# Gathers of a graph attention kernel issued for two edge tiles at a time

## The reference

```python
# reference(), shortened
xn = _layernorm(x, axis=-1)
x = x + gnn(xn, src, dst, ...) + mix(xn[None], ...)[0]
x = x + ffn(_layernorm(x, axis=-1)[None], ...)[0]

# gnn: N = 3125 nodes, 103125 edges sorted by dst, H = 4 heads of D = 64
q = (feat @ Wq).reshape(N, H, D)
k = (feat @ Wk).reshape(N, H, D)
v = (feat @ Wv).reshape(N, H, D)
e = jnp.einsum('ehd,ehd->eh', k[src], q[dst]) / sqrt(H * D)
ex = jnp.exp(e - segment_max(e, dst)[dst])
a = ex / segment_sum(ex, dst)[dst]
ft2 = segment_sum(v[src] * a[..., None], dst).reshape(N, F)
rst = _layernorm(ft2 + feat, ln_g, ln_b)
...                       # two layers with a leaky unit, a second layernorm
# mix: per head of 32 features, sums over tokens of products of pairs of
# normalised k with v, then the same pairs of normalised q against them
# ffn: router, top 2 of 8 experts, gelu(xe @ W1 + b1) @ W2 + b2
```

## Time and profile before

| | |
|---|---|
| median of 3 runs | 2643.17 us |
| lowest and highest | 2631.5 and 2644.66 us |
| the profiled execution, its time | 2620.13 us |
| its span in the profile | 2618.4 us |
| TensorE clock granted, mean share of full speed | 0.851 |
| busy in the span: PE, DVE, ACT, POOL | 2074.0, 1757.7, 1479.9, 1215.0 us |
| first and last gather of the edges start | 107.7 and 1726.5 us |

### The profile page before, as it was taken

One profiled execution on the slowest core, in us unless ns is written; L12 is line 12 of the kernel. 1 busy time (PEld: TensorE's weight loads), 2 busy tenths in 40 slices (PEclk: granted clock), 3 DMA queues, 4 the chain that ended last, 5 costly groups with the idle time before them and its releaser, 6 DMA issues. The chain is left out here.

```text
span 2618.4 us, 45726 instructions
## 1 busy us (share of the span) xinstructions
PE 2074.0 (79%) x12641; PEld 1454.6 (56%) x12641; DVE 1757.7 (67%) x3515; ACT 1479.9 (57%) x4918; POOL 1215.0 (46%) x1183
## 2 busy tenths in 40 slices
PE   7747777777786667778777777857989986999998
PEld 3423333333332255556555555545778876999997
DVE  7457777777777676676667566677979985444443
ACT  2246555665665636566566555666865534555554
POOL 0456555555566445555555555524820001444443
PEclk9868788888888758787888877867989987999999
DMA  7666666666666556666666556647920118222221
GB/s 215 201 181 201 189 187 183 197 186 194 186 195 198 173 161 178 175 191 177 195 177 192 176 169 196 188 125 228 313 95 25 31 42 288 38 35 35 33 36 20
DMA packets 227731, 406.06 MB, mean 155 GB/s; under 512 B 58972, under 2 KB 129809, under 8 KB 227521
## 3 DMA queue, kind: packets, MB, share of 16 engines
q0 software_dynamic: 83712, 250.84, 34.5%
q1 hardware_dynamic: 120852, 116.88, 14.9%
q10 hardware_dynamic: 22957, 35.95, 3.7%
HBM read 345.66 MB, written 58.83 MB: 154 GB/s over the span
## 5 line engine op out<-in xcount | busy, mean ns | idle before, releaser
L826 POOL DMA_INDIRECT ring<-kv_tab,idx x904 | 918.4, 1016 | 709.0 <-issue 361.3
L1170 ACT ACTIVATE val<-ring,val 128x64 f32<-128x64 f32 x1808 | 477.2, 342 | 8.2 <-DVE part L928 7.3
L885 DVE TENSOR_TENSOR ring<-ring,tile_bank 128x1024 f32<-128x1024 f32 x226 | 274.4, 1214 | 64.5 <-ACT tile_bank L1160 41.6
L890 DVE TENSOR_REDUCE score<-ring 128x16 f32<-128x1024 f32 x226 | 268.3, 1212 | 0.0
L922 DVE TENSOR_TENSOR val<-val 128x1040 f32<-128x1040 f32 x113 | 140.3, 1242 | 184.0 <-ACT val L1170 174.5
L1286 PE MATMUL tile_bank<-q_win,spread 128*128 128x256 f32 x452 | 176.2, 476 | 108.3 <-DVE val L914 50.6
L2240 POOL DMA_INDIRECT out<-e_yw,to_row x56 | 120.7, 2155 | 222.3 <-DVE e_yw L2267 206.1
L2316 PE MATMUL e_h<-e_xT,e_now 128*128 128x128 f32 x1792 | 211.9, 277 | 0.7 <-DVE e_now L2257 0.7
L2316 PEld LDWEIGHTS e_h<-e_xT,e_now 128*128 128x128 f32 x1792 | 207.2, 194 | 1.1 <-DVE e_now L2257 1.1
L2331 PE MATMUL e_yps<-e_now,e_hT 128*128 128x256 f32 x896 | 202.5, 379 | 0.0
L2225 POOL DMA_INDIRECT xr<-rows,from_row x56 | 57.5, 1027 | 289.8 <-issue 289.5
(11 more groups left out here) (424 smaller groups left out, 5004.7 us busy)
## 6 DMA issues: line engine op xcount, KB each, us to landing
g_ring<-parts SPq DMA_DIRECT2D x137, 260.0 KB, 4.4
parts<-part ACTq DMA_DIRECT2D x113, 260.0 KB
q_win<-q_tab SPq DMA_DIRECT2D x226, 128.0 KB
e_w_all<-L_ffn_W SPq DMA_DIRECT2D x16, 1024.0 KB, 11.7
ring<-kv_tab,idx POOLq DMA_INDIRECT x904
kv_tab<-kv_t SPq DMA_DIRECT2D x25, 224.0 KB
blocks<-t SPq DMA_DIRECT2D x216, 5.0 KB
blocks<-t SPq DMA_DIRECT2D x216, 0.0 KB
```

The costliest lines, as they stand in the source:

```text
L826: pool.indirect_dma_start(out=ring[:, n % RING, g * L + e, :], out_offset=None, in_=t.kv_tab, in_offset=bass.IndirectOffsetOnAxis(ap=idx[n ...
L885: dve.tensor_tensor(k, k, bcast(q_ps[g].unsqueeze(1), 128, L, F), ALU.mult).then_inc(q_read[g], 1)
L890: dve.tensor_reduce(score[:, :, g, :], ring[:, n % RING, g * L:(g + 1) * L, 0:F].rearrange("p s (h d) -> p s h d", h=HG), AX.X, ALU.add).t ...
L1170: one = act.activation(val[n % 2][:, 1, e, h, 0:DG], ring[:, n % RING, L + e, F + h * DG:F + (h + 1) * DG], ACT.Copy, scale=val[n % 2][:, ...
```

## The change

POOL now takes two tiles at a time. Before an even tile n it waits until `idx_ready` covers tile n + 1 as well, and until `val_ready` and `act_val_ready` both say that tiles n - 4 and n - 3 have left the ring. Then it adds one to `carrier` and issues the gathers of tile n and of tile n + 1, sixteen in all, with no wait between them. The last tile, 112, is alone. What is gathered, where it goes and which semaphores count it stay the same, as do the programs of all other engines.

```diff
             for n in range(TILES):
-                pool.wait_ge(idx_ready, n + 1)
+                if n % 2 == 0:
+                    both = min(n + 2, TILES)
+                    pool.wait_ge(idx_ready, both)
+                    wait(pool, val_ready, both - RING)
+                    wait(pool, act_val_ready, both - RING)
+                    pool.sem_inc(carrier, 1)
                 for g in range(G):
-                    wait(pool, (val_ready, act_val_ready)[g], n - RING + 1)
-                    pool.sem_inc(carrier, 1)
                     for e in range(L):
                         pool.indirect_dma_start(...)
```

## The result

| | changed | before | ratio, 95% interval |
|---|---|---|---|
| the measurement predicted | 2890.53 us (2888.92 to 2892.68, 4 runs) | 2639.59 us (4 runs) | 1.099 [1.095, 1.103] |
| repeat, chip A | 2895.22 us | 2627.95 us | 1.102 [1.096, 1.108] |
| repeat, chip B | 2893.65 us | 2622.21 us | 1.103 [1.096, 1.111] |
| repeat, chip C | 2900.95 us | 2626.09 us | 1.107 [1.099, 1.115] |

The change costs 10%, 251 us in the first measurement. The forecast was 2758 us, slower by 115, with a range up to 2890. The direction and the place of the loss were right; the size was less than half of what came.

What follows compares the result with a forecast made beforehand. The edges were held bound by other engines' stops late in gather runs. Terms 0 + 1 + 0 + 113 + 0 = 114 us onto the profiled 2620.1 us gave 2734, median 2758 us; range 2615 to 2890 us.

Steps and rivals of the forecast that it cites:

- What bounds the kernel: Stage of the edges: other engines stop late in a run of back-to-back gathers, and a stop tends to last until its end.
- No landings late: Later gathers in the edges: a pair's first gather waits for both groups of tile n - 3; costed at 0.
- margin of 1.4 us at tile 26: Tightest place found: landing expected at 495.9, with 2.7 us from gather end to DVE's release; DVE wanted it at 497.31.
- Fewer waits on POOL: Three of four waits and increments go for each pair; worth 0 since POOL waits for ACT, otherwise some 0.3 us each.
- The first tile and the removed waits: Stage opening: first gather also waits for tile 1's row numbers, 1 us taken, bounds 0 and 7.6; removed waits worth 0.
- The second kind of tile: Edges after the first half, 31.5 pairs: one 15.5 us stop replaces 11.9 us ACT idle, +3.6 us a pair, +113 us.
- nearly all of it is stops: Step for the edges' second half: ACT's idle time, 6.0 us a tile or 11.9 a pair, taken as nearly all stops.
- The first kind of tile: First half of the edges, 23 pairs: 11.0 us stop against 11.0 us ACT idle, 0 us, bounds -51 and +53 us.
- No change: Rival: existing runs of sixteen average 29.0 us apart, as two tiles take today, so time stays 2643 us; chance 0.17.
- Faster: Rival: one stop per pair replaces two; at 27.5 us a pair, 54 pairs gain 81 us, 2562 us; chance 0.15.
- Landings late: Rival: landings become late besides the longer stops, 1.6 us a pair, 86 us onto the forecast, some 2845 us; chance 0.07.
- does not do what it says: Rival: POOL itself is stopped in the run; ruled out by 32 gathers at 1.27 us each, given no chance.

Runs made afterwards that it cites:

- one-pause kernel: Changed kernel plus one POOL wait between a pair's two tiles until the first tile's eight gathers landed: 2647.04 us, ratio 1.011, chip B; 2384.98 us, 1.068, chip D.
- paced kernel before: Kernel before plus a 128x128 clear on POOL and a wait for it behind every gather: 2473.74 us, ratio 0.944, chip B; 2474.73 us, 1.109, chip D.
- kernels with pauses: Changed kernel plus POOL waits for landings, behind every four gathers (2853.32 us, ratio 1.086) or once in each pair (2647.04 us on B, 2384.98 us on D).
- paced changed kernel: Changed kernel plus a 128x128 clear on POOL and a wait for it behind every gather: 2482.60 us, ratio 0.947; on chip D 2395.28 us, 1.074.
- half step: Kernel before with one wait per tile for both groups' places, then eight gathers: 2711.11 us, ratio 1.035, chip C; 2230.19 us, 1.000, chip D.

## Why the prediction was right and wrong

**What bounds the kernel: right.** The stage is bound by stops late in a run of gathers. The one-pause kernel showed it (runs halved, 247 of 271 us back), and so did the paced kernel before (not a wait removed, 5.6% faster than before). That POOL's waits are harmless for what POOL delivers was right too.

**No landings late: right.** L888 waited 2.0 us in the whole run. The margin of 1.4 us at tile 26 was reckoned too wide, though: in the kernels with pauses it took 3.4 to 3.9 us from the end of a gather to the engine that waited for it, and not 2.7, which leaves 0.2 to 0.7 us.

**Fewer waits on POOL: not seen, rightly so**, since POOL waits for ACT anyway. Where POOL is the bound, a place to wait cost 0.54 us, and not the 0.3 that I named.

**The first tile and the removed waits: right**, as far as can be told. The first gather waited 8.5 us for its row numbers, against 7.60, so +0.9 against +1. It starts at 110.0 in place of 107.7; the rest came before it.

**The second kind of tile: the mechanism right, the term mis-sized.** I forecast a stop of 15.5 us a pair in place of 11.9 us of ACT's idle time, +3.6 us for each of 31.5 pairs, 113 us. I summed from the timeline of ACT all its idle times over 2.5 us. In the stretch from 1200 to 1800 us these are 269.9 us over 33 tiles, 16.4 a pair; in the stretch of before from 1000 to 1640 us they are 217.1 over 43, 10.1 a pair. The size of the new stop was near: behind 912 us the longest gap begins 7.5 us into the run at the median, and the last one ends at 22.9, against 4.9 and 22.0; all long gaps of a pair make 16.4 us against 15.5. The step that failed is "nearly all of it is stops": of the 11.9 us a pair only 10.1 were long gaps, and the short ones between them stayed where they were. After the change ACT's idle time is 18.3 us a pair, of which 16.4 are long gaps. So 0.9 us was missing in the stop and 1.8 us was subtracted too much, which makes 6.3 in place of 3.6. Measured over all tiles behind the first stretch, of which there are 65 and not 63, it is (1117 / 64 - 928 / 65) x 2 = 6.4 us a pair, +206 us. Here 928 us runs from 830 to the last part at 1758.2 before, and 1117 us from 912 to 2029.1.

**The first kind of tile: wrong.** I gave it 0, from 11.0 us of stop in place of 11.0 us of idle time, with bounds of 51 and 53 us. It cost 732 / 47 - 650 / 46 = 1.44 us a tile, 66 us for the 46, outside of the upper bound. It is the same failed step. The long gaps are 291.2 us over 47 tiles now, 12.4 a pair, and were 205.6 over 46, 8.9 a pair. So the long gaps came to 1.4 us more than my middle value, and 2.1 us of short gaps had been counted as if they were stops and would go; ACT's work took 0.5 us a pair less. Nor is it one stop here: the longest gap of a pair has 7.9 us on average out of the 12.4. Its median onset, 9.5 us, was inside the 8.7 to 13.2 that I took. I also took the clump of 1.6 us off the stop in the second kind and not in the first. With it the forecast would have been 37 us lower (23 x 1.6), and farther off.

113 and 0 became 206 and 66, together 272 us, beside the 271 us by which the last part moved. ACT's "remote" grew by 264 us. The stops alone, without any new mechanism, account for the missing half.

**The rivals.** *No change* took runs of sixteen in the trace of before as samples, 29.0 us a pair, and I had noted that they were picked for late stops; the changed kernel's pairs take 31.2 and 36.4 us. Its rule, that fetching instructions is hidden by the rate of issue ("Runtime: NRT & Kernel Launch", "Instruction fetch mechanics", of the Trainium skill), would leave no such stop; on chip D nothing speaks against it; in the profile after engines with work are silent for up to 25.8 us (the longest wait of L1217 above). The instruction packets of the trace after, none of them slow and most silences without one, give no sign of a slow fetch either. Whether fetching is what fails there, no run here shows. *Faster* named the onset that decides, 8.5 us in the second kind and 11.0 in the first. The medians are 7.5 and 9.5, so both came before it, the first by 1 us. The rival shares the failed step, since its 8.5 and 11.0 rest on the same 11.9 and 11.0 us of idle time. *Landings late* and *does not do what it says* did not come about.

**What the signs were.** Of those named ahead, the runs of sixteen with 20.2 us, the single release by ACT's line, the end behind the run, and L885's absence came as said. Others missed their numbers: starts 33 us apart were forecast for the second half and 36 came, 28 to 29 for the first and 31 came, and ACT's idle time was to be near 15 us a pair in the second half and was 18.3.

## What to carry to other kernels

Before you merge waits on an engine that only issues gathers, look at what the other engines do while it issues: a wait that looks idle may be what lets them run. Where a cost replaces idle time, subtract only the gaps of its own kind, read one by one; the total of an engine's idle time also holds the short gaps that stay. And a gather queue with spare time can be worth slowing: a small instruction and a wait behind every second gather made this kernel 6.7% faster on a chip that has the stops. On one that has none, spacing every gather cost 10.9%, so such a step has to be measured on both.

## What was not expected of the hardware

- Chips differ: the same program takes 2231 us on one and 2622 to 2628 us on three others. The whole difference lies in the stage with dense gathers, and with the paced kernel before (2474.73 and 2473.74 us) it is gone. With the paced changed kernel 87 us of it are left (2395.28 and 2482.60). Which of a kernel's changes pay depends on it: the half step costs 3.5% on C and nothing on D, the spaced gathers gain 5.6% on B and cost 10.9% on D. I know of no version here that is best on both.
- Half the bytes don't shorten a stop: with half rows the share of the DMA engines fell from 0.57 to 0.34 and the time stayed, 2891.82 and 2893.65 us.
- In a stop PE goes on at a crawl, one or two matmuls each 1.4 us in the row from 1613 us, with the cause "issue"; ACT had nothing for 16.91 us.
- Four gathers in 5.9 us in place of 5.0 to 5.5, with a clear and a wait behind each or each second one, were enough to take about two thirds of the stops away (ACT's "remote" from 344 us to 109 and 124). The mean pace accounts for that. A kernel with the same pace and no waits of POOL for its own work was not run.
- A stop shows under many names: "remote" for ACT's next instruction, ACT's line for DVE's. What it is inside the chip stays open.
